# Second stage of a two-layer image kernel: the per-pixel channel contraction is collected densely in one PSUM bank

## The chip, the cores and the metric

One core of a Trainium2 chip runs the whole kernel. The metric is the device time of one execution in microseconds (us); the figure given for the kernel is the median of three runs.

## The reference, cut to what matters

The input `x` has 16 images of 64 channels, 256 x 256 pixels each, in float32 (16 MB an image). Two layers each add a convolution-like term of the normalised image to it:

```python
x = x + L0(_gn(x))     # FFT, mix 16 channels in each of 4 heads on 32 x 17 modes, inverse FFT, + bias
x = x + L1(_gn(x))     # at each pixel, over the 64 channels:
#   alpha = xf[:, 0] * mu[0] - xf[:, 1:] @ mu[1:]     (mu: one vector for the whole batch)
#   alpha = max(alpha, 1 + EPS);  d = arccosh(alpha);  var = mean(d * d)
#   coef = d / sqrt(alpha * alpha - 1);  v = coef * (x - alpha * mu);  ... scaled by 1 / sqrt(var)
```

`_gn` normalises over pairs of channels. The part that this change touches is `alpha`: one weighted sum over 64 channels for each of the 65,536 pixels of an image. The normalised input of layer 1 is x plus a low-frequency field, so the sum splits in two: a weighted sum of the raw x (from DRAM), and the same sum taken on the 32 x 17 modes and brought back to pixels by a small inverse transform.

## The kernel before, in words

The kernel has three stages with a barrier between them. Stage A computes transforms and statistics, stage B (`stage_b`) computes for each pixel the maps derived from `alpha`, and stage C reads x once more and writes the output. Only stage B is changed.

Stage B reads every image once more. An image is cut into T = 8 tiles of 2 MB, `xt`, in NX = 4 buffers: partition p = 2c + s holds half s of channel c, 4096 pixels to a tile. SP issues the loads (`load(b, t)`, L632), and each waits until the tile that had its buffer has been contracted (`al_mm`).

- **PE.** `contract(b, t)` (L650) makes 8 matmuls of 128x512 float32 with a 32-column stationary operand `awc` (weights in columns 0 and 1, one for each half s, zeros in the rest), four into each of two PSUM banks `p_al[k]`, at partitions 0, 32, 64 and 96. Only 2 of the 32 result rows of each carry data. `layer(b)` stands between tiles 6 and 7: the inverse transform along h into `p_z` (L659), a copy by ACT (`zs`), then along w into `p_y[0]` (the alpha part) and `p_y[1]` (channel 0's field), L666.
- **ACT.** `copy_alpha` (L692) copies each bank to `al_r`, twice for a tile; `store_alpha` (L697) writes the rows with data to DRAM (`alx`) after tiles 3 and 7. Between tiles 3 and 4 of image b it runs `distances(b - 1)` (L707 to L715): two square roots, a logarithm and a squared sum, each waiting for DVE.
- **DVE.** For image b: `combine(b)` (L804 to L810) multiplies and sums the modes `spt` (loaded from `spec`) for the layer, then `dense(b - 1)` (L824 to L850) computes the maps of the image before on 128x512 tiles, from `ald` (alpha read back from `alx`) and `x0d` (channel 0). Channel 0 and the maps are laid out with image rows on partitions.
- **POOL.** It issues the small DMAs, in this order for image b: `weights(b)` (L741, waits until image b - 1 is contracted), `load_modes(b)` (L747, two DMAs into the only `spt`), `load_dense(b - 1)` (`x0d`, then `ald` once `alx` is written), `store_dense(b - 1)` (L760 to L762: `maps`, `bmap`, `x10`).

```python
            with dve.Fori(1, B) as b:
                ch.loop(b, 1, PER_B)
                combine(b)
                dense(b - 1)
                ch.end(B - 1)
```

Before the loop DVE runs `combine(0)` and then a long setup of the weights of stage C (L856 to L911). What POOL, SP and PE of one image wait for is counted by semaphores; the order on each engine is the order of the code.

Of the kernel before, what the change touches and what calls it, by code (L numbers as in the profile page):

```python
# [36 lines left out]
def constants():  # L37
# [28 lines left out]
    c["idft_h"] = ih  # L66
    w = 2 * np.pi * ky[:, None] * np.arange(W) / W
# [481 lines left out]
def stage_b(nc, ctx, io, B, keep):  # L549
# [3 lines left out]
    SL = T * TB // (4 * 512)  # L553
    x_v = x.rearrange("b c h w -> b (c h w)").rearrange("b (p t n) -> b t p n", p=128, t=T)
    x0_v = x.rearrange("b c (s h) w -> b c h s w", s=2)
    al_v = io["alx"].rearrange("b s (h w) -> b h s w", w=W)
    al_rows = io["alx"].rearrange("b s (k j n) -> b s j k n", j=4, n=512)
# [3 lines left out]
    al_mm, al_sb = sem("al_mm"), sem("al_sb")  # L561
    al_out = [sem(f"al_out{k}") for k in range(2)]
    al_in, x0_in, sp_in, sp_used = sem("al_in"), sem("x0_in"), sem("sp_in"), sem("sp_used")
# [7 lines left out]
    with ExitStack() as mem:  # L571
# [3 lines left out]
        al_r = sb("al_r", [128, SL, 512])  # L575
# [11 lines left out]
        aw, awc = sb("aw", [128, B, 32]), sb("awc", [128, 32])  # L587
# [10 lines left out]
        ald, x0d, x10, al, t1, t2, w1, w2, dist, coef, beta = (dn[:, k] for k in range(11))  # L598
# [11 lines left out]
        def _(sp):  # L610
# [14 lines left out]
            sp.dma_start(idft_h[:], cst["idft_h"]).then_inc(c_in, 16)  # L625
# [15 lines left out]
        def _(pe):  # L641
            def contract(b, t):

                pe.wait_ge(x_in[t % NX], b * (16 * T // NX) + (t // NX) * 16 + 16)
                for k in range(2):
                    if not (is_at(b, 0) and t == 0):
                        pe.wait_ge(al_sb, b * 2 * T + 2 * t + k - 1)
                    for j in range(4):
                        at = 2048 * k + 512 * j
                        last = nc.tensor.matmul(p_al[k][32 * j:32 * j + 32, :], awc[:], xt[t % NX][:, at:at + 512], start=True, stop=True)  # L650
                    last.then_inc(al_mm, 1)

            def layer(b):
# [8 lines left out]
                if not is_at(b, 0):  # L662
                    pe.wait_ge(alpha, b * 2)
# [20 lines left out]
        def _(act):  # L684
            S = nc.scalar

            def copy_alpha(b, t):
                for k in range(2):
                    act.wait_ge(al_mm, b * 2 * T + 2 * t + k + 1)
                    if t % (T // 2) == 0 and k == 0 and not is_at(b, 0):  # L690
                        act.wait_ge(al_out[2 * t // T], b * 32)
                    S.activation(al_r[:, 2 * t + k], p_al[k][:], ACT.Copy).then_inc(al_sb, 1)  # L692

            def store_alpha(b, half):
                act.wait_ge(al_sb, b * 2 * T + (half + 1) * T)
                for s in range(2):
                    act.dma_start(al_rows[b, s][:, half * T:half * T + T], al_r[s::32, half * T:half * T + T]).then_inc(al_out[half], 16)  # L697

# [688 lines left out]
```

## Time and profile before

| | |
|---|---|
| median of 3 runs | 4943.81 us (4943.03 to 4945.26) |
| profiled execution, its span | 4939.4 us |
| stage A | 0 to 1351.4 us of the span |
| stage B | 1351.4 to 2266 us |
| stage C | 2266 to 4939.4 us |
| PE / DVE / ACT / POOL busy over the span | 77% / 69% / 45% / 30% |
| DMA over the span | 242 GB/s on average |

The profile is of one execution. Its span runs from the first to the last instruction and is 4.4 us under the median of the runs. "Idle before, releaser" tells how long an engine had nothing to do before a group and what ended that. A matmul of float32 shows as more than one record. [...]

### The profile page before, as it was taken

The numbers are of one execution on the slowest core, as the hardware profiler recorded it, in microseconds if no ns is written. First come the engines' busy times: TensorE is split into PE (matmuls) and PEld (weight loads), VectorE is DVE, ScalarE is ACT, GpSimd is POOL, SyncE is SP. The second block draws the span as 40 slices with busy tenths as digits, with TensorE's granted clock in tenths as the row PEclk, the third lists the DMA queues.
The fourth block names the chain that finished last, engine by engine and source line by source line (L and its number), as shares of the span: only waits on it lengthen the run. The fifth ranks groups of instructions, "written<-read, shape, count | busy, mean of one in ns | idle before, by whom it ended". The sixth has DMA issues, their size and how long they took to land.

```text
span 4939.4 us, 72319 instructions
## 1 busy us (share of the span) xinstructions
PE 3805.1 (77%) x23619; PEld 2097.6 (42%) x23874; DVE 3399.5 (69%) x3499; ACT 2240.3 (45%) x3020; POOL 1460.1 (30%) x737
## 2 busy tenths in 40 slices
PE   7777777777144344433999999999999999999998
PEld 3444444444111011002555555555555555555554
DVE  2989889898863433343776677667767776676677
ACT  5555555455022233232554455445554554454544
POOL 0010110101100010001454444444444444444444
PEclk9988888898566677766999999999999999999999
DMA  9565756655099989982777777777777777777776
GB/s 367 192 251 188 258 198 229 228 193 213 14 381 357 364 342 363 351 345 81 224 235 219 227 239 221 224 223 241 224 222 224 237 227 224 227 234 224 223 244 217
DMA packets 288845, 1197.47 MB, mean 242 GB/s; under 512 B 30174, under 2 KB 46846, under 8 KB 205828
## 3 DMA queue, kind: packets, MB, share of 16 engines
q1 hardware_dynamic: 274740, 1151.85, 68.7%
q0 software_dynamic: 11600, 38.32, 2.1%
q10 hardware_dynamic: 2304, 4.20, 0.2%
q8 instruction: 178, 2.92, 0.2%
q14 instruction: 23, 0.19, 0.0%
HBM read 883.32 MB, written 310.94 MB: 242 GB/s over the span
## 4 chain that ended last, share of the span: by engine, by line
PE 50%; issue 3%; DMA 1%; DVE 0%; SPq 0%; POOL 0%; ACT 0%; POOLq 0%; ACTq 0%
PE c_p_u L1129 20%; PE c_p_z L1099 11%; PE c_p_t L1112 10%; PE c_p_p L1153 5%; PE c_p_g L1135 4%; DMA c_mv<-bmap 0%; POOL c_ot L1306 0%; ACT c_zc L1189 0%; DVE c_zc L1280 0%; DMA c_ys<-spec 0%; SPq L1070 0%; DMA c_x<-x 0%; DVE c_rt L1288 0%; SPq L1069 0%; PE c_p_z L1174 0%
## 5 line engine op out<-in xcount | busy, mean ns | idle before, releaser
L1306 POOL TENSOR_TENSOR c_ot<-c_s,c_u 128x1024 f32<-128x1024 f32 x512 | 1211.3, 2366 | 1411.6 <-DVE c_s L1259 1411.6
L1189 ACT ACTIVATE c_zc<-c_p_z 34x512 f32<-34x512 f32 x512 | 546.4, 1067 | 1316.0 <-PE c_p_z L1099 1261.5
L1250 DVE TENSOR_TENSOR c_u<-c_xt,c_p_u 128x1024 f32<-128x1024 f32 x512 | 625.3, 1221 | 745.0 <-PE c_p_u L1129 722.5
L1129 PE MATMUL c_p_u<-c_mv,c_zc 128*128 128x256 f32 x4096 | 1043.7, 399 | 76.5 <-issue 75.5
L1129 PEld LDWEIGHTS c_p_u<-c_mv,c_zc 128*128 128x128 f32 x4096 | 750.7, 193 | 590.1 <-issue 465.7
L650 PE MATMUL b_p_al<-b_xt,b_awc 128*32 128x512 f32 x2048 | 333.9, 791 | 502.6 <-ACT b_al_r L692 314.9
L1259 DVE SCALAR_TENSOR_TENSOR c_s<-c_u,keep_k,c_p_g 128x1024 f32<-128x1024 f32 x512 | 655.8, 1281 | 18.0
L1269 DVE TENSOR_TENSOR c_ot<-c_ot,c_p_p 128x1024 f32<-128x1024 f32 x512 | 621.4, 1214 | 1.8 <-POOL c_ot L1306 1.3
L1218 ACT ACTIVATE c_sq<-c_s,c_btcol 128x1024 f32<-128x1024 f32 x512 | 589.2, 1151 | 52.8 <-DVE c_s L1259 22.3
L1099 PEld LDWEIGHTS c_p_z<-c_idft_h,c_ys 128*34 128x34 f32 x8176 | 477.6, 113 | 224.7 <-issue 215.2
L1099 PE MATMUL c_p_z<-c_idft_h,c_ys 128*34 128x64 f32 x8176 | 559.6, 222 | 7.8 <-ACT c_zc L1189 7.8
L329 ACT ACTIVATE a_junk<-a_xt 128x1024 bf16<-128x1024 f32 x512 | 534.4, 1049 | 31.1 <-DMA a_xt<-in_x 23.7
L1112 PE MATMUL c_p_t<-c_sq,c_halves 128*32 128x512 f32 x2048 | 538.7, 605 | 0.0
L248 PE MATMUL a_p_rows<-a_xt,a_dft_h 128*64 128x512 f32 x2048 | 504.5, 638 | 34.2 <-DMA a_bias_t<-in_bias 19.6
L391 DVE TENSOR_REDUCE a_y<-a_prod 128x34 f32<-128x1088 f32 x256 | 502.7, 2005 | 5.7
L336 ACT ACTIVATE a_rows<-a_p_rows 128x512 f32<-128x512 f32 x256 | 151.4, 591 | 532.9 <-PE a_p_rows L248 532.9
L650 PEld LDWEIGHTS b_p_al<-b_xt,b_awc 128*32 128x32 f32 x2048 | 65.0, 130 | 760.7 <-ACT b_al_r L692 426.9
L804 DVE TENSOR_TENSOR b_prod<-b_spt,b_arow 64x2176 f32<-64x2176 f32 x16 | 38.7, 2418 | 474.6 <-DMA b_spt<-spec 474.2
L515 POOL TENSOR_TENSOR a_sm<-a_sm 128x8 f32<-128x8 f32 x16 | 26.8, 1675 | 1138.1 <-DVE a_sm L452 1138.1
L692 ACT ACTIVATE b_al_r<-b_p_al 128x512 f32<-128x512 f32 x256 | 149.3, 595 | 404.6 <-PE b_p_al L650 404.5
L386 DVE TENSOR_TENSOR a_prod<-a_wm,a_xh 128x1088 f32<-128x1088 f32 x256 | 317.9, 1283 | 0.3
L261 PE MATMUL a_p_tr<-a_ident,a_rows 128*128 128x128 f32 x1024 | 163.5, 297 | 189.1 <-DVE a_cols L374 177.1
(177 smaller groups left out, 3090.8 us busy)
## 6 DMA issues: line engine op xcount, KB each, us to landing
a_xt<-in_x SPq DMA_DIRECT2D x256, 1024.0 KB, 9.7
b_xt<-in_x SPq DMA_DIRECT2D x128, 2048.0 KB, 18.9
c_xt<-in_x SPq DMA_DIRECT2D x256, 1024.0 KB, 6.4
out<-c_ot SPq DMA_DIRECT2D x256, 1024.0 KB, 8.5
maps<-b_maps POOLq DMA_DIRECT2D x16, 768.0 KB, 14.9
c_rt<-maps SPq DMA_DIRECT2D x256, 48.0 KB
a_wm<-in_wmix SPq DMA_DIRECT2D x1, 8704.0 KB, 34.9
b_spt<-spec POOLq DMA_DIRECT2D x32, 272.0 KB, 23.4
```

Of the source, the lines that this page charges most:

```text
L248: last = nc.tensor.matmul(p_rows[i][64 * t:64 * t + 64, :], dft_h[:, j], xt[q % NX][:, t::2, i, j * W:(j + 1) * W], start=(j == 0), stop=( ...
L329: nc.scalar.activation(junk[h % 2][:].rearrange("p (i w) -> p i w", i=2), xt[q % NX][:, h], ACT.Square, accum_out=sq[:, q, h:h + 1]).then_ ...
L391: ch.inc(V.tensor_reduce(y[:, o].rearrange("p (a k) -> p a k", a=2), prod[o % 2][:].rearrange("p a (n k) -> p a k n", k=KY), AX_X, ALU.add))
L1099: last = nc.tensor.matmul(p_z[0:M2, 64 * c:64 * c + 64], ys[:, 8 * part + c], idft_h[:].rearrange("p (s h) -> p s h", s=2)[:, :, 32 * chun ...
L1112: last = nc.tensor.matmul(p_t[at:at + 32, :], halves[:], sq[n][:, 512 * j:512 * j + 512], start=True, stop=True)
L1129: ins = nc.tensor.matmul(p_u[:, W * r:W * r + W], zc[ck % 2][:, (t % TCH) * ROWS + row], mv[t % 2][:, W * row:W * row + W], start=True, st ...
L1189: S.activation(zc[chunk_buffer][0:M2, :, 16 * part:16 * part + 16].rearrange("m h c -> m c h"), p_z[0:M2, :].rearrange("m (c h) -> m c h", ...
L1218: S.activation(sq[n][:], s0[n][:], ACT.Square, bias=btcol[:]).then_inc(sq_done, 1)
L1250: V.tensor_tensor(u[n][:], xt[t % 4][:, 1024 * n:1024 * n + 1024], p_u[:], ALU.add).then_inc(u_done, 1)
L1259: V.scalar_tensor_tensor(out=s0[n][:], in0=u[n][:], scalar=keep["k"][:], in1=p_g[:], op0=ALU.mult, op1=ALU.mult).then_inc(s_done, 1)
L1269: V.tensor_tensor(o, o, p_p[:], ALU.add).then_inc(o_done, 1)
L1306: P.tensor_tensor(ot[t % 4][:, 1024 * n:1024 * n + 1024], s0[n][:], u[n][:], ALU.add).then_inc(v_done, 1)
```

## The change

- `contract` writes all matmuls of an image into one bank `p_al`, four column groups as before. The stationary operand is a window of 32 columns of a 47-column `awc` that has weights in columns 15 and 31: for pixel block k the window starts at 15 - k, so the two data rows land on rows k and 16 + k of each group, and the other rows get zeros added. After 16 blocks the bank holds the alpha of all pixels of the image, dense. The first block starts the accumulation, the rest add to it.
- The layer's alpha part is accumulated into the same bank; channel 0's field goes to one bank `p_y`. A reordered constant, `idft_d`, gives both in the new order of pixels.
- `copy_alpha`, `store_alpha`, the `alx` tensor, `ald` and the waits on them are gone. DVE reads `p_al` itself and counts `al_read`; PE waits for it before tile 0 of the next image. There is one `p_al` where there were two banks used in turn.
- `dense` starts with the operation on `p_al` (one operation fewer); ACT's work for an image is `copy_z(b)`, then `distances(b)`.
- Channel 0, `maps`, `bmap` and `x10` are moved in four DMAs of 32 partitions instead of one of 128; runs in DRAM are twice as long. `load_dense(b)` is now issued in image b's own turn, after `load_modes(b)`.

```diff
             def load(b, t):
                 if not (is_at(b, 0) and t < NX):
-                    sp.wait_ge(al_mm, b * 2 * T + 2 * (t - NX) + 2)
+                    sp.wait_ge(al_mm, b * T + t - NX + 1)
                 sp.dma_start(xt[t % NX][:], x_v[b, t]).then_inc(x_in[t % NX], 16)
...
                 pe.wait_ge(x_in[t % NX], b * (16 * T // NX) + (t // NX) * 16 + 16)
-                for k in range(2):
-                    if not (is_at(b, 0) and t == 0):
-                        pe.wait_ge(al_sb, b * 2 * T + 2 * t + k - 1)
-                    for j in range(4):
-                        at = 2048 * k + 512 * j
-                        last = nc.tensor.matmul(p_al[k][32 * j:32 * j + 32, :], awc[:], xt[t % NX][:, at:at + 512], start=True, stop=True)
-                    last.then_inc(al_mm, 1)
+                if t == 0 and not is_at(b, 0):
+                    pe.wait_ge(al_read, b)
+                for e in range(8):
+                    k, j = 2 * t + e // 4, e % 4
+                    last = nc.tensor.matmul(p_al[32 * j:32 * j + 32, :], awc[:, 15 - k:47 - k], xt[t % NX][:, 512 * e:512 * e + 512],
+                                            start=(k == 0), stop=False, skip_group_check=True)
+                last.then_inc(al_mm, 1)
...
-                for q in range(2):
-                    for s in range(2):
-                        last = nc.tensor.matmul(p_y[q][:, 256 * s:256 * s + 256], zs[:, q, 128 * s:128 * s + 128], idft_w[0:M2], start=True, stop=True)
+                for r in range(2):
+                    nc.tensor.matmul(p_y[:, 256 * r:256 * r + 256], zs[:, 1, HD * r:HD * r + HD], idft_w[0:M2], start=True, stop=True)
+                for r in range(2):
+                    last = nc.tensor.matmul(p_al[:, 256 * r:256 * r + 256], zs[:, 0, HD * r:HD * r + HD], idft_w[0:M2],
+                                            start=False, stop=False, skip_group_check=True)
...
             def entry(b):
-                for t in range(T):
-                    copy_alpha(b, t)
-                    if t == T // 2 - 1:
-                        store_alpha(b, 0)
-                        if not is_at(b, 0):
-                            distances(b - 1)
-                    if t == T - 2:
-                        copy_z(b)
-                store_alpha(b, 1)
+                copy_z(b)
+                distances(b)
...
             def load_dense(b):
                 if not is_at(b, 0):
-                    pool.wait_ge(alpha, b * 2)
-                pool.dma_start(x0d[:].rearrange("p (s w) -> p s w", s=2), x0_v[b, 0]).then_inc(x0_in, 16)
-                for half in range(2):
-                    pool.wait_ge(al_out[half], b * 32 + 32)
-                pool.dma_start(ald[:].rearrange("p (s w) -> p s w", s=2), al_v[b]).then_inc(al_in, 16)
+                    pool.wait_ge(alpha, b)
+                for j in range(4):
+                    pool.dma_start(x0d[32 * j:32 * j + 32], x0_v[b, 0, j]).then_inc(x0_in, 16)
...
             def store_dense(b):
                 pool.wait_ge(maps_ready, b + 1)
-                pool.dma_start(io["maps"][b].rearrange("m s (h w) -> h (m s) w", w=W), maps[:].rearrange("p m (s w) -> p (m s) w", s=2)).then_inc(maps_out, 16)
-                pool.dma_start(io["bmap"][b].rearrange("s (h w) -> h s w", w=W), beta[:].rearrange("p (s w) -> p s w", s=2)).then_inc(beta_out, 16)
-                pool.dma_start(io["x10"][b].rearrange("s (h w) -> h s w", w=W), x10[:].rearrange("p (s w) -> p s w", s=2)).then_inc(x10_out, 16)
+                for j in range(4):
+                    at = slice(32 * j, 32 * j + 32)
+                    pool.dma_start(maps_v[b, j], maps[at]).then_inc(maps_out, 16)
+                    pool.dma_start(dense_v(io["bmap"])[b, j], beta[at]).then_inc(beta_out, 16)
+                    pool.dma_start(dense_v(io["x10"])[b, j], x10[at]).then_inc(x10_out, 16)
...
             def entry(b):
                 weights(b)
                 load_modes(b)
-                load_dense(b - 1)
+                load_dense(b)
                 store_dense(b - 1)
...
-                V.scalar_tensor_tensor(out=x10[:], in0=x0d[:], scalar=brow[:, 0:1], in1=p_y[1][:], op0=ALU.add, op1=ALU.add).then_inc(alpha, 1)
-                V.tensor_tensor(t1[:], ald[:], p_y[0][:], ALU.add).then_inc(alpha, 1)
-                dve.wait_ge(alpha, b * 2 + 2)
-                ch.step(V.tensor_scalar(al[:], t1[:], col(ac, b), 1.0 + EPS, ALU.add, ALU.max))
+                V.tensor_scalar(al[:], p_al[:], col(ac, b), 1.0 + EPS, ALU.add, ALU.max).then_inc(al_read, 1)
+                V.scalar_tensor_tensor(out=x10[:], in0=x0d[:], scalar=brow[:, 0:1], in1=p_y[:], op0=ALU.add, op1=ALU.add).then_inc(alpha, 1)
+                dve.wait_ge(al_read, b + 1)
```

## Rows read from the trace of the kernel before

**Rows 1.** Stage B: busy of PE, PEld, DVE, ACT, POOL; clock, DMA share, GB/s.

```profile
1351.40:2269.00 917.60, 381.80 (x2242) 94.20 (x2242) 386.21 (x431) 260.93 (x399) 90.20 (x136) 0.70 0.88 341
```

**Rows 2.** Waits, stage B: engine, line, releaser: total us, times, longest.

```profile
DVE b_prod L804 <- DMA b_spt<-spec: 474.2, 15, 34.2
...
PE b_p_al L650 <- ACT b_al_r L692: 314.9, 46, 20.3
```

**Rows 3.** Combine's first multiply, by source line: duration, first and last start.

```profile
L804 DVE TENSOR_TENSOR b_prod<-b_spt,b_arow x16: 2417/2418/2419, 1383.2 to 2207.7; 64x2176 f32<-64x2176 f32 x16
```

**Rows 4.** Timeline, steady period: start, us, engine, line, operation, [idle before <- releaser].

```profile
1515.78 24.97 SPq L632 DMA_DIRECT2D b_xt<-in_x  x7
...
1523.21 0.21 POOL L741 COPY b_awc<-b_aw 128x32 f32 x1 [1.93 <-PE b_p_al L650]
...
1523.94 1.22 POOL L747 DMA_DIRECT2D b_spt<-spec  x2 [0.53 <-issue]
...
1536.76 3.39 PE L650 MATMUL b_p_al<-b_xt,b_awc 128*32 128x512 f32 x16 [4.70 <-DMA b_xt<-in_x]
...
1551.20 2.42 DVE L804 TENSOR_TENSOR b_prod<-b_spt,b_arow 64x2176 f32<-64x2176 f32 x1 [33.11 <-DMA b_spt<-spec]
...
1558.77 0.75 DVE L824 SCALAR_TENSOR_TENSOR b_dn<-b_dn,b_brow,b_p_y 128x512 f32<-128x512 f32 x1 [0.70 <-DMA b_dn<-alx]
...
1566.53 5.58 PE L650 MATMUL b_p_al<-b_xt,b_awc 128*32 128x512 f32 x32 [18.16 <-ACT b_al_r L692]
...
1572.04 1.05 PE L659 MATMUL b_p_z<-b_idft_h,b_vm 128*34 128x256 f32 x4
...
1577.83 0.20 POOL L741 COPY b_awc<-b_aw 128x32 f32 x1 [1.92 <-PE b_p_al L650]
```

**Rows 5.** Two windows of that period; columns as in rows 1.

```profile
1508.00:1512.00 4.00, 0.12 (x4) 0.12 (x8) 3.93 (x4) 3.83 (x7) 0.00 (x0) 0.50 0.86 365
1512.00:1516.00 4.00, 4.00 (x20) 0.82 (x24) 3.86 (x7) 1.32 (x3) 0.00 (x0) 0.52 0.12 49
```

**Rows 6.** DMA issues, stage B: count, KB, median us to landing.

```profile
b_spt<-spec POOLq DMA_DIRECT2D x32, 272.0 KB, 23.4
...
x<-b_dn POOLq DMA_DIRECT2D x16, 256.0 KB, 21.2
```

**Rows 7.** Tile view of xt: its matmuls (ns; first, last start), landing times.

```profile
L650 PE MATMUL b_p_al<-b_xt,b_awc x2048: 592/617/1063, 1370.9 to 2232.9; 128*32 128x512 f32 x187
...
DMA to landing us min/median/max: 7.2/18.9/29.4
```

**Rows 8.** Timeline of the start of stage B, image 0.

```profile
1368.85 1.18 POOL L747 DMA_DIRECT2D b_spt<-spec  x2
...
1383.17 2.42 DVE L804 TENSOR_TENSOR b_prod<-b_spt,b_arow 64x2176 f32<-64x2176 f32 x1 [8.99 <-DMA b_spt<-spec]
...
1384.91 3.64 PE L650 MATMUL b_p_al<-b_xt,b_awc 128*32 128x512 f32 x16 [3.08 <-DMA b_xt<-in_x]
...
1399.60 3.48 PE L650 MATMUL b_p_al<-b_xt,b_awc 128*32 128x512 f32 x16 [2.97 <-DMA b_xt<-in_x]
```

**Rows 9.** Timeline of image 1's combine and image 0's dense.

```profile
1442.69 2.42 DVE L804 TENSOR_TENSOR b_prod<-b_spt,b_arow 64x2176 f32<-64x2176 f32 x1 [0.33 <-DVE keep_lw L869]
...
1449.97 0.75 DVE L824 SCALAR_TENSOR_TENSOR b_dn<-b_dn,b_brow,b_p_y 128x512 f32<-128x512 f32 x1 [0.41 <-DVE b_sc L810]
```

**Rows 10.** Timeline: end of stage B, first operation of stage C.

```profile
2231.54 1.92 PE L650 MATMUL b_p_al<-b_xt,b_awc 128*32 128x512 f32 x16
...
2243.03 0.75 DVE L824 SCALAR_TENSOR_TENSOR b_dn<-b_dn,b_brow,b_p_y 128x512 f32<-128x512 f32 x1 [14.12 <-DMA b_dn<-alx]
...
2258.05 1.04 POOL L760 DMA_DIRECT2D maps<-b_maps  x1 [17.54 <-issue]
...
2259.79 0.73 POOL L762 DMA_DIRECT2D x<-b_dn  x1
...
2266.11 3.55 POOL L1323 MEMSET c_mv<- 128x2048 f32 x2 [4.98 <-POOLq L571]
```

More of the change, by code:

```diff
@@ L552, in stage_b @@
     NX, T = 4, HALF // TB
-    SL = T * TB // (4 * 512)
+    HD = 128
     x_v = x.rearrange("b c h w -> b (c h w)").rearrange("b (p t n) -> b t p n", p=128, t=T)
-    x0_v = x.rearrange("b c (s h) w -> b c h s w", s=2)
-    al_v = io["alx"].rearrange("b s (h w) -> b h s w", w=W)
-    al_rows = io["alx"].rearrange("b s (k j n) -> b s j k n", j=4, n=512)
+    x0_v = x.rearrange("b c (q j r) w -> b c j q (r w)", j=4, r=2)
+    dense_v = lambda a: a.rearrange("b s (k j n) -> b j (s k) n", j=4, n=512)
+    maps_v = io["maps"].rearrange("b m s (k j n) -> b j (s k) m n", j=4, n=512)
     x_in = [sem(f"x_in{k}") for k in range(NX)]
@@ L560, in stage_b @@
     mm_done, pow_done, mean_ready = sem("mm_done"), sem("pow_done"), sem("mean_ready")
-    al_mm, al_sb = sem("al_mm"), sem("al_sb")
-    al_out = [sem(f"al_out{k}") for k in range(2)]
-    al_in, x0_in, sp_in, sp_used = sem("al_in"), sem("x0_in"), sem("sp_in"), sem("sp_used")
+    al_mm, al_read = sem("al_mm"), sem("al_read")
+    x0_in, sp_in, sp_used = sem("x0_in"), sem("sp_in"), sem("sp_used")
     v_ready, z_mm, z_sb, y_mm = sem("v_ready"), sem("z_mm"), sem("z_sb"), sem("y_mm")
@@ L586, in stage_b @@
         arow = sb("arow", [128, B, C])
-        aw, awc = sb("aw", [128, B, 32]), sb("awc", [128, 32])
+        aw, awc = sb("aw", [128, B, 2]), sb("awc", [128, 47])
         ac, q2, q3, dsum = sb("ac", [128, B]), sb("q2", [128, B]), sb("q3", [128, B]), sb("dsum", [128, B])
@@ L597, in stage_b @@
         dn = sb("dn", [128, 11, 512])
-        ald, x0d, x10, al, t1, t2, w1, w2, dist, coef, beta = (dn[:, k] for k in range(11))
+        _, x0d, x10, al, t1, t2, w1, w2, dist, coef, beta = (dn[:, k] for k in range(11))
         wide = dn[:, 4:8].rearrange("p k n -> p (k n)")[:, 0:2 * B * C].rearrange("p (b c s) -> p b c s", b=B, s=2)
@@ L602, in stage_b @@
         maps = sb("maps", [128, 6, 512], BF16)
-        p_al = [ps(f"p_al{k}", [128, 512]) for k in range(2)]
+        p_al = ps("p_al", [128, 512])
         p_z = ps("p_z", [128, 512])
-        p_y = [ps(f"p_y{k}", [128, 512]) for k in range(2)]
+        p_y = ps("p_y", [128, 512])
         p_v = ps("p_v", [128, 512])
@@ L685, in _ @@
             S = nc.scalar
[L687 to L697, printed above, removed]
             def copy_z(b):
@@ L731, in _ @@
                 entry(b)
-            distances(B - 1)
         @block.gpsimd
@@ L739, in weights @@
                 if not is_at(b, 0):
-                    pool.wait_ge(al_mm, b * 2 * T)
-                P.tensor_copy(awc[:], aw[:, b]).then_inc(w_ready, 1)
+                    pool.wait_ge(al_mm, b * T)
+                P.tensor_copy(awc[:, 15:47:16], aw[:, b]).then_inc(w_ready, 1)
             def load_modes(b):
@@ L778, in _ @@
             load_modes(0)
+            load_dense(0)
             pool.wait_ge(uw_ready, 1)
@@ L872, in _ @@
             ch.inc(V.memset(btrow[:, 0:1], 0.0))
-            ch.inc(V.memset(aw[:], 0.0))
+            ch.inc(V.memset(awc[:], 0.0))
             ch.inc(V.memset(vm[:], 0.0))
@@ L1340, in program @@
         io["macc"] = dram("macc", (HEADS, CI))
-        io["alx"] = dram("alx", (B, 2, HALF))
         io["x10"] = dram("x10", (B, 2, HALF))
```

26 lines of the change are left out of this document (13 added, 13 removed).

## Prediction, written before the changed kernel ran

> **What bounds the kernel now.** I read the windows by stage first. Stage B, the only one that the change touches, is a third of the work in length but has DMA busy for 0.88 of its time at 341 GB/s, while PE is busy for 382 of 918 us and DVE for 386 [rows 1]. That looks like a stage bound by its loads. Two further views say that this is not the whole answer. In the waits, DVE stands for 474 us before combine because the modes `spt` have not landed, up to 34 us at a time, and PE stands for 315 us behind ACT's copies [rows 2]. And in each period there is a hole: of two windows of 4 us one has DMA at 0.86, the next at 0.12 [rows 5], which makes 4.1 us without loads.
>
> The period is 54.6 us: combine of image 1 starts at 1442.7 [rows 9], that of image 15 at 2207.7 [rows 3], 14 periods in 765 us. The timeline of one period shows what closes it [rows 4]. I call t0 the end of an image's last contraction, just before `weights` at 1523.2.
> - t0 to the start of combine, 28.1 us: POOL waits for t0 before `load_modes`; its two DMAs are issued by 1525.2 and have landed at 1551.2.
> - combine to PE's restart, 15.3 us: combine, `dense` of the image before, and ACT's `distances` inside its row of copies (1551.2 to 1566.5).
> - restart to the next t0, 11.2 us: two tiles in 5.6 us, then layer and one tile in another 5.6.
>
> The sum is 54.6. So the period is a ring of latencies, PE to POOL to DMA to DVE to ACT to PE, that happens to stand close to what the loads need. After the restart only tiles 5 to 7 are left to contract, and all of them are in their buffers.
>
> **The change, part by part.**
>
> *ACT's copies, `alx`, `ald` go.* 256 copies, 64 stores and 16 loads. The 15.3 us section loses what stood behind ACT: it now ends with the first operation of `dense`. What DVE does in combine stays. The `alx` traffic (0.26 MB written and read for each image, beside some 19 MB) is worth 1 or 2 us of DMA time in a period; as the new ring is not filled by DMA, I count it as nothing, and it would count if DMA closed the ring.
>
> *The new wait.* PE may not start tile 0 of image b before DVE has read `p_al` of b - 1. DVE's order is combine(b), dense(b - 1). combine(b) needs `spt` of b, whose load POOL issues only after t0 of b - 1. So the whole of an image's contraction now lies behind the landing of its modes; before, tiles 0 to 4 of it ran in that time. Behind the waiting PE stand SP's loads, since a buffer comes free only by a contraction: four tiles are loaded ahead, and then the load queue dries out. The new ring has four terms. S is the moment when PE starts an image.
>
> 1. S to t0, all eight tiles. Tiles 0 to 3 are there. The first takes 3.6 us at the lower clock, 0.50 after the wait [rows 5, 8]; then tile 4 is issued, at S + 3.9. A load into an idle queue takes 7.2 us at least [rows 7], so it lands at S + 11.1. Undisturbed, tiles follow 4.9 us apart (three from 1384.9 to 1399.6) [rows 8]. Beside POOL's stores they take 6.9: three tiles from the issue at 1515.8 to 1536.8 are 21.0, less 7.2, over two [rows 4]. The stores start some 13 us after S (`dense` takes 15.0 us to its first store [rows 10], less what went before S). I take 4.9 for tile 5, 6.9 for 6 and 7: tile 6 lands at S + 22.9. Its contraction takes 3.6 us; layer and tile 7 take 5.6 at the full clock [rows 4], and I take 8.1 at the lower one, as 3.64 against 1.92 us for the tile alone says [rows 8, 10]. That makes 34.6 us. Ends: 28.4 with 4.9 throughout and a full clock, 36.6 with 6.9 throughout.
> 2. t0 to the issue of the second `spt` DMA: 2.1 us, as now [rows 4].
> 3. Its landing. With an empty POOL queue but x loads beside it: 13.1 us (1370.0 to 1383.2) [rows 8]. Behind the three stores: 26.0 us [rows 4]. In the new order the stores are issued from S + 13 and t0 comes at S + 35, so they have 22 us; now the last of them lands 21.2 us after its issue [rows 6]. They are just about through. I take 15, near the lower end, with 13.1 and 26.0 as ends.
> 4. combine, 7.6 us (1551.2 to 1558.8) [rows 4], then the read of `p_al`, one operation not above 0.75 [rows 4], and its signal: 8.4 us. No end is far from it.
>
> The period is 34.6 + 2.1 + 15 + 8.4 = 60.1 us, 5.5 more than now. All low ends together give 52.0, all high ends 73.1.
>
> *The stores in four parts.* Twelve DMAs in place of three, and four for channel 0. An issue of this size costs POOL 0.6 us (1.22 for two) [rows 4], so about 7 us in place of 2.5. In the ring this lies between S + 13 and S + 22, before t0, and costs nothing; if t0 came before S + 22, `weights` and `spt` would be late by it. At the end of the stage nothing covers it.
>
> [...] The parts are 64 KB, those of `maps` 192 KB. The rows have nothing smaller than the 64 KB of `alx`, and no effect of its size can be read from the rows above. [...]
>
> *Matmuls.* As many as before, same shape, same four column groups; only where they write and that they add. I cost this at nothing; the bound above is that adding to one bank keeps the groups from overlapping, a rival below. The window of `awc` and the layer's new order change no size.
>
> *First and last image.* `combine(1)` still starts at 1442.7, since the setup of stage C's weights sets it [rows 9]; `dense(0)` starts at 1450.0, so S of image 1 is 1450.8. At the end, the trip over `alx` goes: now t0 at 2233.5 is followed by `dense` at 2243.0, its first store at 2258.05, the last at 2259.8, and stage C at 2266.1 [rows 10]. Then: t0 + 0.3, `dense` to the stores 14.3 (15.0 less the dropped 0.7), 7 us of issues, and 5.6 from there to stage C: 27.2 us in place of 32.6.
>
> **The sum.** S of image 15 is 1450.8 + 14 x 60.1 = 2292.2; t0 is 2326.8; stage C starts at 2354.0 instead of 2266.1, 87.9 us later. Stages A and C are the same work. The profiled execution's own time, 4939.4, becomes 5027.3. The median of the runs stands 4.4 us above that span: 5031.7. A microsecond of period is 14 us of time, and the change breaks even at a period of 53.8 us.
>
> **The rivals.**
> - *The buffers hide the wait (faster).* If four loaded tiles carry DMA over PE's wait, DMA closes the ring: 54.6 less the hole of 4.1 is 50.5 us, stage C starts at 2219.6, and the time is 4897. It needs PE back within about 18 us of t0, while tiles 1 to 3 of the next image still land (three at 6 us). For it speaks the high DMA share; against it that term 3 and 4 alone make 23.4, and with both at their low ends still 21.5. It decides at a period under 53.8, so nearly all low ends must come together. 8 in 100.
> - *A milder ring.* Loads less disturbed, `spt` at 13: period 55.5, time 4967. 9 in 100.
> - *POOL's queue is slower in parts.* If the stores in parts are not through when `spt` is issued, `spt` lands in 20 us instead of 15, halfway to the present 26: period 65.1, stage C at 2424, time 5102. For it: POOL's DMAs do wait for each other and for x loads, 13.1 against 26.0. [...] Against it: the stores have 22 us. 17 in 100.
> - *Column groups no longer overlap.* 16 records of 0.617 us for a tile [rows 7] one after another are 9.9 us, eight tiles and the layer some 85 us, period 110, time about 5790. Nothing in the rows speaks for it. 2 in 100.
> - *The likeliest*, period 57 to 63: 4988 to 5074. 60 in 100. The rest, 4 in 100, is what I have not thought of.
>
> **How the numbers follow.** The time is 5032. For 8 in 10 I go from a period of 56.1 to the queue rival: 4975 to 5105. Differences under 0.2%, 10 us, can't be told from none here; a period of 53.1 to 54.5 would give that. Faster by more: 0.09. Within: 0.03. Slower by more: 0.88.
>
> **What would show it.** In the profile after: PE's longest waits ended by DVE's first operation of `dense`, 15 times and some 25 us each with the rest of idle time on DMA; DMA at nothing for about 10 us of each period, share in stage B near 0.8; combine 60 us apart; `spt` landing about 15 us after its issue; layer at tile 6 not waiting. DVE's wait for `spt` stays the largest. The prediction is wrong if the x queue never dries, if t0 comes later than S + 37 (tiles slower than 6.9), or if `spt` lands as late as now.

## The result and the profile after

| | median | runs | against the kernel before |
|---|---|---|---|
| kernel before | 4943.42 us | 4935.26 to 4945.26, 4 runs | |
| changed kernel | 4976.59 us | 4969.14 to 4979.09, 4 runs | 1.0068, 95% interval 1.0053 to 1.0082 |

The change makes the kernel 33 us slower. The forecast was slower by 88 us: the direction is right, the size is 2.7 times too large. The median lies 1.6 us inside the low end of the forecast range (4975 to 5105). The profiled execution took 4969.1 us with a span of 4967.6, the shortest of its four runs, so its span shows 28 us where the medians show 33.

The windows by stage of the changed kernel (columns as in [rows 1]):

```profile
1351.40:2295.00 943.60, 382.50 (x2242) 103.24 (x2242) 375.42 (x410) 93.81 (x128) 157.96 (x307) 0.67 0.83 323
```

Stage B is 26 us longer in these bounds (stage C starts 30.9 us later, see below), with DMA at 0.83 and 323 GB/s where [rows 1] have 0.88 and 341. ACT's work fell from 261 to 94 us and the bytes fell too, and the stage is longer all the same. Two waits of stage B, from the view of waits (columns as in [rows 2]):

```profile
DVE b_prod L785 <- DMA b_spt<-spec: 505.7, 15, 36.8
...
PE b_p_al L648 <- DVE b_dn L805: 372.3, 15, 34.8
```

PE's wait for ACT's copies [rows 2] has gone. In its place stands a wait for DVE's first operation of `dense` (L805), once for each of images 1 to 15, 25 us on average. DVE's own wait for the modes is longer than before, 506 us against 474. One whole period in the timeline of the changed kernel:

```profile
1563.93 9.45 PE L648 MATMUL b_p_al<-b_xt,b_awc 128*32 128x512 f32 x64 [23.69 <-DVE b_dn L805]
...
1575.12 1.92 PE L648 MATMUL b_p_al<-b_xt,b_awc 128*32 128x512 f32 x16 [1.74 <-DMA b_xt<-in_x]
...
1580.02 1.93 PE L648 MATMUL b_p_al<-b_xt,b_awc 128*32 128x512 f32 x16 [2.97 <-DMA b_xt<-in_x]
...
1585.72 3.60 PE L648 MATMUL b_p_al<-b_xt,b_awc 128*32 128x512 f32 x16 [3.78 <-DMA b_xt<-in_x]
...
1589.25 1.05 PE L658 MATMUL b_p_z<-b_idft_h,b_vm 128*34 128x256 f32 x4
...
1593.09 3.37 PE L648 MATMUL b_p_al<-b_xt,b_awc 128*32 128x512 f32 x16
...
1596.69 0.19 POOL L722 COPY b_awc<-b_aw 128x2 f32 x1 [12.64 <-PE b_p_al L648]
1597.40 1.21 POOL L728 DMA_DIRECT2D b_spt<-spec  x2 [0.53 <-issue]
1611.66 2.42 DVE L785 TENSOR_TENSOR b_prod<-b_spt,b_arow 64x2176 f32<-64x2176 f32 x1 [35.25 <-DMA b_spt<-spec]
...
1619.11 0.75 DVE L805 TENSOR_SCALAR b_dn<-b_p_al,b_ac 128x512 f32<-128x512 f32 x1 [0.58 <-DVE b_sc L791]
...
1620.01 8.72 PE L648 MATMUL b_p_al<-b_xt,b_awc 128*32 128x512 f32 x64 [23.54 <-DVE b_dn L805]
```

It is to be read as the ring of the forecast. PE starts at 1563.9 right behind the read of `p_al`, contracts four tiles that were there, then takes tiles 4 to 6 as they land (1575.1, 1580.0, 1585.7), the layer, and tile 7. t0 is at 1596.5; `weights`, then the two DMAs of the modes; they have landed 13.1 us after the last issue; combine; the read; PE starts at 1620.0. The terms are 32.6 + 2.1 + 13.1 + 8.3 = 56.1 us, where the ring before took 54.6 [rows 3, 4, 9]. Two sections got shorter: t0 to combine 15.2 us instead of 28.1, combine to PE's restart 8.3 instead of 15.3, where PE had stood behind ACT. The third, restart to t0, grew from 11.2 to 32.6, since all eight tiles lie in it now, and that is more than the two saved. Combine's first multiply gives the mean: image 1's starts at 1441.6, image 15's at 2229.4, so 56.3 us for each of 14 periods. From the view by source line:

```profile
L785 DVE TENSOR_TENSOR b_prod<-b_spt,b_arow x16: 2416/2416/2418, 1382.1 to 2229.4; 64x2176 f32<-64x2176 f32 x16
```

and from the timeline, image 1:

```profile
1441.64 2.42 DVE L785 TENSOR_TENSOR b_prod<-b_spt,b_arow 64x2176 f32<-64x2176 f32 x1 [0.33 <-DVE keep_lw L850]
```

How long the DMAs of the modes take to land, over all images, from the tile view of `spt`:

```profile
DMA to landing us min/median/max: 9.3/12.5/15.8
```

Windows of 4 us of that period (columns as in [rows 5]): the first two hold the layer and tile 7, the last three, at the end of the period, show the dry load queue:

```profile
1588.00:1592.00 4.00, 3.32 (x17) 1.27 (x10) 0.00 (x0) 1.64 (x2) 0.00 (x0) 0.84 0.96 402
1592.00:1596.00 4.00, 4.00 (x21) 1.11 (x19) 0.00 (x0) 0.23 (x1) 0.00 (x0) 0.58 1.05 446
...
1612.00:1616.00 4.00, 0.00 (x0) 0.00 (x0) 3.97 (x2) 0.00 (x0) 0.00 (x0) 0.50 0.78 332
1616.00:1620.00 4.00, 0.00 (x0) 0.02 (x1) 3.35 (x5) 0.00 (x0) 0.00 (x0) 0.50 0.00 0
1620.00:1624.00 4.00, 3.99 (x24) 1.18 (x28) 3.80 (x7) 2.48 (x3) 2.02 (x4) 0.58 0.15 47
```

In the last 12 us DMA stands for 8.3 by its shares (0.22, 1.00 and 0.85 of 4 us), against 4.1 before [rows 5]. The end of the stage in the timeline of the changed kernel:

```profile
2237.75 8.75 PE L648 MATMUL b_p_al<-b_xt,b_awc 128*32 128x512 f32 x64 [24.67 <-DVE b_dn L805]
...
2270.71 0.75 DVE L805 TENSOR_SCALAR b_dn<-b_p_al,b_ac 128x512 f32<-128x512 f32 x1 [20.47 <-PE b_p_al L648]
...
2284.28 0.59 POOL L741 DMA_DIRECT2D maps<-b_maps  x1 [26.42 <-DVE b_maps L831]
...
2290.05 0.50 POOL L743 DMA_DIRECT2D x<-b_dn  x1
...
2297.01 3.55 POOL L1304 MEMSET c_mv<- 128x2048 f32 x2 [5.86 <-POOLq L571]
```

`dense` of the last image now follows its contraction at once (before: 9.5 us later, over `alx` [rows 10]). Twelve stores take POOL 6.3 us. Stage C starts at 2297.0 instead of 2266.1, 30.9 us later; stage C itself is 2.7 us shorter in this execution.

### The profile page after: what moved, and what is told of

It is laid out like the page before. It is cut to its first block, busy times and chain, and to the rows that moved or that the text cites. A ratio compares the mean times of both kernels' runs of the same rounds, so it can differ in the third digit from the quotient of the medians.

```text
span 4967.6 us, 72010 instructions
## 1 busy us (share of the span) xinstructions
PE 3854.0 (78%) x23874; PEld 2112.6 (43%) x23874; DVE 3391.0 (68%) x3483; ACT 2070.9 (42%) x2749; POOL 1529.9 (31%) x913
## 4 chain that ended last, share of the span: by engine, by line
PE 51%; issue 1%; DMA 0%; DVE 0%; SPq 0%; ACT 0%; POOLq 0%; DVEq 0%; ACTq 0%
PE c_p_u L1110 20%; PE c_p_z L1080 11%; PE c_p_t L1093 10%; PE c_p_p L1134 6%; PE c_p_g L1116 5%; DMA c_mv<-bmap 0%; DMA c_ys<-spec 0%; ACT c_zc L1170 0%; DVE c_zc L1261 0%; SPq L1051 0%; DMA c_x<-x 0%; DVE c_rt L1269 0%; SPq L1050 0%; PE c_p_z L1155 0%; DVE c_ys L1262 0%
## 5 line engine op out<-in xcount | busy, mean ns | idle before, releaser
L1134 PE MATMUL c_p_p<-c_rt,keep_lw 128*128 128x512 bf16 x1024 | 310.2, 385 | 1.9 <-DVE c_ot L1250 1.9
L1116 PE MATMUL c_p_g<-c_rt,keep_lw 128*128 128x512 bf16 x1024 | 310.3, 385 | 0.0
```

Source lines behind the costliest of these rows:

```text
L1116: ins = nc.tensor.matmul(p_g[:, 512 * k:512 * k + 512], lw(0, b), rt[t % 2][:, at:at + 512], start=True, stop=True)
L1134: ins = nc.tensor.matmul(p_p[:, 512 * k:512 * k + 512], lw(1, b), rt[t % 2][:, at:at + 512], start=True, stop=True)
```

## Experiments

Two theories stood against each other. *The wait*: the loss is PE's wait for the read of `p_al`, which stands on DVE behind a combine whose modes are loaded only after the contraction, and so the load queue runs dry. *The parts*: the loss is in the small DMAs. A third, slower matmuls into one bank, was tested along. Differences are between the medians, each to runs of the kernel before taken with it (medians 4938.3 to 4941.5 us); the changed kernel is at +33.

| run | median | difference | ratio, 95% interval |
|---|---|---|---|
| modes_early | 4859.56 us | -79 | 0.9841 (0.9825 to 0.9858) |
| dense_first | 4852.81 us | -85 | 0.9829 (0.9813 to 0.9845) |
| two_banks | 4863.83 us | -78 | 0.9843 (0.9826 to 0.9859) |
| unrolled | 4977.44 us | +36 | 1.0069 (1.0054 to 1.0084) |
| modes_twice | 5102.21 us | +161 | 1.0325 (1.0308 to 1.0342) |
| before_parts | 5010.23 us | +72 | 1.0145 (1.0128 to 1.0162) |
| before_no_alx | 4913.89 us | -24 | 0.9949 (0.9933 to 0.9966) |
| first_modes_twice | 4919.67 us | -22 | 0.9952 (0.9935 to 0.9968) |
| first_extra_plain | 4924.71 us | -17 | 0.9961 (0.9946 to 0.9977) |
| first_extra_wide | 4881.62 us | -60 | 0.9875 (0.9860 to 0.9890) |
| first_stores_twice | 4944.96 us | +3 | 1.0011 (1.0001 to 1.0020) |
| best | 4837.58 us | -104 | 0.9795 (0.9781 to 0.9808) |

### modes_early: the modes are loaded before they are waited for

In POOL's `entry(b)`; the modes of image 1 are loaded after `load_dense(0)`:

```diff
                 weights(b)
-                load_modes(b)
                 load_dense(b)
+                if not last:
+                    load_modes(b + 1)
                 store_dense(b - 1)
```

> Changed kernel, with one reordering on POOL: the modes of the next image are loaded right after channel 0's, before the stores, and no longer after the end of the image's contraction. If the lost time is PE's wait for the read of p_al behind combine and the modes' landing (about 15.5 us from the last contraction to combine), combine is done before the contraction ends, PE restarts about 1 us after it, the load queue never runs dry, and the period falls from 56.3 us to what DMA needs, 48 to 51 us: about 80 to 110 us less than the changed kernel, near 4880, and faster than the kernel before. If the loss is the bytes or the number of the small DMAs, they are the same here: period 55 to 57, time within 15 us of the changed kernel. If it is slower matmuls into one bank, the same.

Measured: 79 us under the kernel before, 112 under the changed one. A window inside stage B (columns as in [rows 1]) has DMA at full share:

```profile
1480.00:2060.00 580.00, 335.83 (x1688) 76.20 (x1690) 238.49 (x265) 70.35 (x97) 116.21 (x228) 0.70 1.01 395
```

The small DMAs, the bytes and the matmuls are those of the changed kernel. The wait carries the loss. The time is some 20 us under what was expected: DMA closes the period at 47.2 us, not at 48 to 51.

### dense_first: the order on DVE

```diff
-                combine(b)
                 dense(b - 1)
+                combine(b)
```

> Changed kernel, with one reordering on DVE: in the loop dense(b - 1) comes before combine(b); the modes are still loaded after the contraction's end. If PE's wait is one of order (the read of p_al stands behind combine), PE restarts 1 us after the last contraction and the period falls to 48 to 51 us, time near 4880, although the modes land as late as before. If the landing of the modes by itself closes the ring (through the layer at tile 6), the period stays above 54 and the time above 4940.

Measured: 85 us under the kernel before, with the modes loaded as late as in the changed kernel. In its timeline PE's tile 0 follows the last contraction with the read between them, 1.1 us of idle time:

```profile
1569.52 1.92 PE L648 MATMUL b_p_al<-b_xt,b_awc 128*32 128x512 f32 x16
...
1571.61 0.75 DVE L805 TENSOR_SCALAR b_dn<-b_p_al,b_ac 128x512 f32<-128x512 f32 x1 [24.78 <-PE b_p_al L648]
...
1572.37 1.21 POOL L728 DMA_DIRECT2D b_spt<-spec  x2 [0.53 <-issue]
...
1572.51 1.92 PE L648 MATMUL b_p_al<-b_xt,b_awc 128*32 128x512 f32 x16 [1.07 <-DVE b_dn L805]
```

So it is not the landing by itself, nor the one bank by itself, but the order: the read of `p_al` had no need of combine(b) and stood behind it. From here on this kernel serves as a base in which DMA is what closes the period: from 1480 to 2060 its share is 1.01 at 394 GB/s, and image 1 to image 14 take 660.9 us, 47.2 each.

### two_banks and unrolled

```diff
-        p_al = ps("p_al", [128, 512])
+        p_als = [ps(f"p_al{k}", [128, 512]) for k in range(2)]
...
-                if t == 0 and not is_at(b, 0):
-                    pe.wait_ge(al_read, b)
+                p_al = p_als[b % 2]
+                if t == 0 and b > 1:
+                    pe.wait_ge(al_read, b - 1)
```

> Changed kernel with two banks for alpha used in turn by odd and even images, so that tile 0 waits for the read of the image before the last (the loops over images of PE and DVE are written out for it). If the one bank together with the order on DVE makes the wait, PE goes on without it, the load queue does not dry out and the period is 48 to 51 us, time 4850 to 4890. If the late modes stop PE at the layer all the same, the period stays above 54.

`unrolled` has only the loops over images of PE and DVE written out, as two_banks needs them.

> Changed kernel with the loops over images of PE and DVE written out, nothing else: the control for two_banks. Same order, same waits: period 56 to 57 us, time within 15 us of the changed kernel's 4977. If writing them out was what sped two_banks up, it is near 4864.

Measured: two_banks -78 us, unrolled +36, within 3 us of the changed kernel (+33). A second bank takes the wait away as well, and writing the loops out does nothing. `unrolled` also repeats the changed kernel's result.

### modes_twice: a dose of the suspected term

```diff
+                for k in range(2):
+                    pool.dma_start(extra[KX * k:KX * k + KX].rearrange("k (h i) m -> k h (i m)", h=HEADS),
+                                   spec[b, k].rearrange("(h k) n -> k h n", h=HEADS)).then_inc(sp_in, 16)
                 for k in range(2):
                     pool.dma_start(spt[KX * k:KX * k + KX].rearrange("k (h i) m -> k h (i m)", h=HEADS),
```

> Changed kernel, with the modes loaded twice (two more DMAs of the same bytes into a tile of their own, ahead of the real ones). If their landing after the contraction's end is a term of the ring, the period grows by the added landing, from 56.3 to 62 to 67 us, and the time by 80 to 150 us over the changed kernel. If DMA volume closes the ring, the 0.56 MB cost 1.3 us at 430 GB/s: period 57.6, time 20 us over. If neither: no change.

Measured: 128 us over the changed kernel. From its timeline, the issues after t0:

```profile
1621.88 0.19 POOL L723 COPY b_awc<-b_aw 128x2 f32 x1 [12.95 <-PE b_p_al L649]
1622.59 1.21 POOL L729 DMA_DIRECT2D b_extra<-spec  x2 [0.53 <-issue]
1623.79 1.09 POOL L732 DMA_DIRECT2D b_spt<-spec  x2
```

and the landing and PE's restart:

```profile
1645.28 2.42 DVE L789 TENSOR_TENSOR b_prod<-b_spt,b_arow 64x2176 f32<-64x2176 f32 x1 [43.98 <-DMA b_spt<-spec]
...
1653.63 9.75 PE L649 MATMUL b_p_al<-b_xt,b_awc 128*32 128x512 f32 x64 [31.96 <-DVE b_dn L809]
```

The modes land 20.4 us after the last issue instead of 13.1, and 1.1 us more go into issues: 8.4 us a period by these lines. By combine's starts the period is 64.9 us instead of 56.3, 8.6 more, and image 1's combine starts 8.6 us later as well (1450.3), since the setup on DVE stands behind combine(0): 15 times 8.6 are 129. The ring is as drawn.

### before_parts: the stores in parts, alone

`bmap` and `x10` are cut in the same way.

```diff
-                pool.dma_start(io["maps"][b].rearrange("m s (h w) -> h (m s) w", w=W), maps[:].rearrange("p m (s w) -> p (m s) w", s=2)).then_inc(maps_out, 16)
+                for j in range(4):
+                    at = slice(32 * j, 32 * j + 32)
+                    pool.dma_start(io["maps"][b].rearrange("m s (h w) -> h (m s) w", w=W)[at], maps[at].rearrange("p m (s w) -> p (m s) w", s=2)).then_inc(maps_out, 16)
...
```

> Kernel before, with its three stores of 128 partitions cut into twelve of 32, nothing else. POOL's issues take 7 us in place of 2.5, and here they stand right before the contraction's end, so the modes are issued some 2.5 us later: period 57, time about 35 us over the kernel before, if the parts cost nothing in the DMA queue. If the parts hold the queue longer, the modes land more than 26 us after their issue (28 to 31) and the period is 59 to 62, time 60 to 100 us over. If POOL's issues are hidden: no change.

Measured: +72 us, in the second range. Combine's first multiply, by source line:

```profile
L806 DVE TENSOR_TENSOR b_prod<-b_spt,b_arow x16: 2417/2418/2420, 1381.4 to 2271.9; 64x2176 f32<-64x2176 f32 x16
```

Image 1's starts at 1440.9, so the period is 59.4 us, 4.7 more than before; 14 of them make 66 us, and 6 more pass between the last combine and stage C, where twelve issues stand. From its timeline, the first store, tile 7, `weights`, the modes and combine:

```profile
1582.84 0.64 POOL L762 DMA_DIRECT2D maps<-b_maps  x1 [35.40 <-DVE b_maps L852]
...
1586.06 1.92 PE L650 MATMUL b_p_al<-b_xt,b_awc 128*32 128x512 f32 x16
...
1589.86 0.21 POOL L741 COPY b_awc<-b_aw 128x32 f32 x1
...
1590.58 1.20 POOL L747 DMA_DIRECT2D b_spt<-spec  x2 [0.51 <-issue]
...
1619.91 2.42 DVE L806 TENSOR_TENSOR b_prod<-b_spt,b_arow 64x2176 f32<-64x2176 f32 x1 [37.81 <-DMA b_spt<-spec]
```

t0 is at 1588.0, but POOL comes to `weights` only at 1589.9, with its issues between: 1.8 us later than before. From the last modes' issue to combine it is 28.1 us instead of 26.0 [rows 4]. The two tiles after the longer wait take 6.6 us instead of 5.6. That is 4.9 in this period. So behind twelve stores the modes land some 2 us later. Two causes can make that, and the run does not separate them: parts hold the queue longer, or the last store merely has less of a lead, since its issue ends 0.8 us before the modes' begins, where these were 2.7 us in the kernel before. Either way it is far from the 5 us that the queue rival put on the changed kernel, where the stores are issued 20 us ahead and are out of the way when the modes come.

### before_no_alx: what the round trip cost

```diff
-                store_alpha(b, 1)
...
-                pool.dma_start(ald[:].rearrange("p (s w) -> p s w", s=2), al_v[b]).then_inc(al_in, 16)
...
+            ch.inc(V.memset(ald[:], 1.0))
```

> Kernel before, without the writes and the read of alx (alpha is taken as a constant 1 in the maps; copies by ACT stay). It tells what slowed the x tiles to 6.9 us behind PE's restart: if the stores of POOL did it, the third tile still comes 21 us after the first load's issue; if the alx writes did it, 17 to 19 us. The period itself should stay at 53.5 to 54.6 us, since the ring of waits does not pass alx: time within 15 us of the kernel before. If alx traffic was what bound the stage, the period falls by 3 us or more and the time by 45.

Measured: -24 us, outside the 15 that were given for it. From its timeline, the first load after PE's restart, the modes' issue, the third tile and combine:

```profile
1565.70 63.20 SPq L632 DMA_DIRECT2D b_xt<-in_x  x12
...
1574.41 1.21 POOL L743 DMA_DIRECT2D b_spt<-spec  x2 [0.50 <-issue]
...
1585.52 3.64 PE L650 MATMUL b_p_al<-b_xt,b_awc 128*32 128x512 f32 x16 [4.25 <-DMA b_xt<-in_x]
...
1599.80 2.42 DVE L797 TENSOR_TENSOR b_prod<-b_spt,b_arow 64x2176 f32<-64x2176 f32 x1 [31.79 <-DMA b_spt<-spec]
```

The third tile comes 19.8 us after the first issue instead of 21.0, between what the two cases gave, so `alx` accounts for a part of the 6.9 us pace only. The modes land 24.2 us after their last issue instead of 26.0: the round trip did touch the ring, through the modes' landing, by 1.8 us a period (52.8 instead of 54.6 by combine's starts). The forecast had counted this traffic as nothing, on the ground that DMA does not fill the ring; it costs all the same where it delays a landing that is in the ring.

### first_modes_twice, first_extra_plain, first_extra_wide: what slows the tiles

All three on the kernel with dense first, where added DMA time shows in full. The second load of modes is as above; the other two load as many bytes from x, after the modes, first_extra_plain (first lines) into 64 partitions in rows of 8704 B, first_extra_wide (last lines) into 128 in pieces of 2176 B:

```diff
+                for k in range(2):
+                    pool.dma_start(extra[KX * k:KX * k + KX], x_v[0, 0][KX * k:KX * k + KX, 0:C * M2]).then_inc(sp_in, 16)
...
+                for k in range(2):
+                    pool.dma_start(extra[:, 544 * k:544 * k + 544], x_v[0, 0][:, 544 * k:544 * k + 544]).then_inc(sp_in, 16)
```

> The kernel with dense first (period 48.5 us, DMA at full share all through), modes loaded twice: what the modes' load costs the DMA engines. In its windows the rate falls from 430 to 320 GB/s for some 16 us while they are in flight, which makes 4 us lost and 1.3 us for their own bytes: period up by 5.4, time by 80 us. If they cost their bytes alone: 1.3 us, 20 us.

> The kernel with dense first, with an extra load of as many bytes as the modes into the same 64 partitions, in whole rows of 8704 B (from x) instead of pieces of 2176 B. Doubling the modes cost 67 us. If the pieces' size and place in DRAM make them dear, this costs little over its bytes: 20 to 35 us. If it is that 64 partitions are written, that is, half of the memory's width, it costs 55 to 75 us.

> As first_extra_plain, but pieces of 2176 B over all 128 partitions. If the number of partitions makes the modes dear: 20 to 35 us. If the short pieces do: 55 to 75 us.

Measured against dense_first, each by its difference to the kernel before: +64, +69 and +26 us. The first is under the 80 that were expected, the other two fall where "64 partitions" had put them. Not all of this is DMA time in the period. combine(0) waits for the added load too, and the setup on DVE stands behind it, so PE starts image 1 later; the end is longer as well. What images 1 to 14 take, from PE's first matmul of image 1 (timeline) to the last `weights` (tile view of `awc`), in the profiled execution of each:

| run | image 1 starts | last `weights` | 14 images | more, for one image |
|---|---|---|---|---|
| dense_first | 1442.4 | 2103.3 | 660.9 us | |
| first_modes_twice | 1452.0 | 2169.8 | 717.8 us | 4.1 us |
| first_extra_plain | 1451.4 | 2167.4 | 716.0 us | 3.9 us |
| first_extra_wide | 1449.9 | 2128.6 | 678.7 us | 1.3 us |

The runs of one kernel differ by up to 16 us, about 1 us for an image, so 4.1 and 3.9 are the same. 0.56 MB at the 430 GB/s that dense_first moves beside stores (426 to 434 in its windows from 1592 to 1608) are 1.3 us: the wide load costs its bytes, the narrow ones three times as much. With DMA at full share in all of them, the rates say it again, first_extra_plain and then first_extra_wide:

```profile
1480.00:2060.00 580.00, 307.70 (x1544) 69.17 (x1545) 217.61 (x242) 65.18 (x89) 119.45 (x231) 0.69 1.01 372
...
1480.00:2060.00 580.00, 326.90 (x1634) 72.77 (x1636) 237.31 (x264) 68.49 (x94) 130.28 (x252) 0.69 1.01 391
```

So neither the short pieces nor their place in `spec` make the modes dear, but how many partitions the load writes. Two things changed together there and were not separated: the two DMAs of the modes write 64 partitions in all and 32 each, those of the wide load 128 each. The windows of 4 us of dense_first (columns as in [rows 5]) show it from the other side, one with only stores beside the x tiles, then four behind the modes' issue (1573.6), all with DMA near full share:

```profile
1548.00:1552.00 4.00, 2.05 (x12) 0.59 (x16) 0.00 (x0) 0.00 (x0) 0.00 (x0) 0.50 1.05 445
...
1576.00:1580.00 4.00, 2.86 (x16) 0.58 (x16) 3.94 (x2) 2.00 (x4) 0.00 (x0) 0.67 1.05 319
1580.00:1584.00 4.00, 0.64 (x4) 0.00 (x0) 3.83 (x9) 0.00 (x0) 0.00 (x0) 0.91 1.02 299
1584.00:1588.00 4.00, 2.30 (x12) 0.60 (x16) 2.00 (x3) 0.00 (x0) 2.10 (x4) 0.52 1.00 334
1588.00:1592.00 4.00, 1.34 (x8) 0.00 (x0) 3.97 (x2) 0.00 (x0) 3.71 (x8) 0.50 0.99 323
```

The modes have landed at 1587.0. In the last window it is channel 0's four loads of 32 partitions each that can still be in flight: they were issued by 1575.9 and land 15.6 us after their issue in the median. Beside the stores, which read 32 partitions each, the rate holds (426 to 434 GB/s from 1592 to 1608), so they cost about their bytes: tiles 3 to 6 of that image are contracted 5.8 us apart (1592.7 to 1610.1), and these 17.4 us at 430 GB/s are 7.5 MB, three tiles of 2.1 MB and 1.2 of the stores' 1.31 MB.

### first_stores_twice: not conclusive for the stores' price

`bmap` and `x10` are doubled in the same way, to DRAM tensors of their own.

```diff
                     pool.dma_start(maps_v[b, j], maps[at]).then_inc(maps_out, 16)
+                    pool.dma_start(maps2_v[b, j], maps[at]).then_inc(maps_out, 16)
...
```

> The kernel with dense first, maps, bmap and x10 stored twice (24 stores in 32-partition parts): what the stores cost the DMA engines. With only stores beside them the windows show 410 to 455 GB/s and x tiles 5.8 us apart instead of 4.9. If they cost their bytes, 1.31 MB at 430 GB/s: 3 us a period, time up by 45 us. If they had slowed the tiles to 6.9 us, as the forecast's first term has it: 8 to 10 us a period, 120 to 150 us.

Measured: 89 us over dense_first, between the two expectations, and by another cause than either. From its timeline, tiles 5 and 6, `weights`, and the next read of `p_al`:

```profile
1565.44 1.92 PE L649 MATMUL b_p_al<-b_xt,b_awc 128*32 128x512 f32 x16 [2.96 <-DMA b_xt<-in_x]
...
1571.22 3.56 PE L649 MATMUL b_p_al<-b_xt,b_awc 128*32 128x512 f32 x16 [3.85 <-DMA b_xt<-in_x]
...
1580.49 0.19 POOL L723 COPY b_awc<-b_aw 128x2 f32 x1 [4.48 <-PE b_p_al L649]
...
1601.94 0.75 DVE L809 TENSOR_SCALAR b_dn<-b_p_al,b_ac 128x512 f32<-128x512 f32 x1 [32.78 <-DMA x<-b_dn]
```

`dense` waits until the stores of the image before have landed, and with 24 of them that is 21.6 us after t0: a new ring, so the price of the stores can't be taken from the total. What can be read is the pace: tile 6 is contracted 5.8 us after tile 5 with stores in flight, as in the changed kernel (5.7).

### best

`dense(0)` moves between the parts of DVE's setup; SP issues the last image's stores of `bmap` and `x10` after its last load, and POOL keeps those of `maps`.

```diff
+            dense(0)
             ch.step(V.tensor_tensor(v2[:], srow[:, :, 1], over_b(btrow[:]), ALU.add))
...
+            combine(1)
-            with dve.Fori(1, B) as b:
-                ch.loop(b, 1, PER_B)
+            with dve.Fori(2, B) as b:
+                ch.loop(b, 2, PER_B)
                 dense(b - 1)
                 combine(b)
...
+            sp.wait_ge(maps_ready, B)
```

> The kernel with dense first, and two more steps: dense(0) moved into the setup of stage C's weights, so that PE can start image 1 some 25 us earlier (now it waits until about 1443 us, and the load queue runs dry from 1424 on), and the last image's stores of bmap and x10 issued by SP beside POOL's. Period as before, 48 us; the start gains 15 to 22 us, the end 2 to 4: time 4828 to 4836. If the start was hidden (DMA makes up for it later), it stays at 4850.

Measured: 104 us under the kernel before (0.9795), 18 under dense_first, and 2 us over the range that was given; stage C starts at 2158.0 instead of 2176.4. Image 1 starts at 1414.1 instead of 1442.4, but its layer then waits 8.7 us for combine(1), since the setup lies between. From its timeline, image 1's first tile and its layer:

```profile
1414.07 1.92 PE L654 MATMUL b_p_al<-b_xt,b_awc 128*32 128x512 f32 x16 [1.07 <-DVE b_dn L814]
...
1464.08 1.92 PE L664 MATMUL b_p_z<-b_idft_h,b_vm 128*34 128x256 f32 x4 [8.70 <-DVE b_vm L798]
```

## Why the forecast was right in kind and wrong in size

- **The ring.** Right: the four terms are in the trace, and the links that close it were taken out or stretched one by one: the order (dense_first), the landing (modes_early, modes_twice), the bank (two_banks). PE's wait, 15 times and 25 us each, and the dry queue (8.3 us of a period, where 10 were given) are in the profile.
- **The step that failed: the sum of the period, "34.6 + 2.1 + 15 + 8.4 = 60.1".** It measured 56.3. Two of its terms were too large, term 1 by 2.0 us and term 3 by 1.9; terms 2 and 4 came out within 0.1 us.
- **Term 1, 34.6, measured 32.6.** Tiles 4 and 5 came as given, at S + 11.2 and S + 16.1. Tile 6 came at S + 21.8, not 22.9: "Beside POOL's stores they take 6.9" was a wrong reading of [rows 4]. Stores, modes, channel 0's load and `alx` were all in flight in that stretch. Stores alone lift the pace from 4.9 to 5.7 or 5.8 us. `alx` was worth 1.2 us over three tiles (before_no_alx). The modes, dear by the few partitions that they write (3.9 us against 1.3 for as many bytes, first_extra_plain against first_extra_wide), fit the rest; in the kernel before itself they were not taken out. In the changed kernel neither modes nor `alx` are in flight between S and t0. The rest of the term, 0.9 us, is the layer and tile 7: 7.2 us, where 8.1 were taken. The rows named for it, 3.64 against 1.92 us, add 1.7 to the 5.6 and give 7.3; the other 0.8 had no row. The granted clock, a share of the full one, stood at 0.84 and then at 0.58 there, not throughout at 0.50, the lower clock of the forecast (windows above).
- **Term 3, 15, measured 13.1** in the period shown, the lower end: the stores were through. Over all images no DMA of the modes took more than 15.8 us to land. What the queue rival feared of the parts is at most some 2 us right behind twelve stores (28.1 for 26.0 us, before_parts), where its cause was not separated, and here nothing; no run shows that DMA takes longer over a store for its being cut into parts of 64 or 192 KB.
- **How it adds up.** The 14 periods took 787.8 us where 14 x 60.1 = 841.4 were given, 53.6 less. Image 1 started 0.8 us earlier than given, the last image's term 1 was 1.9 shorter (2237.8 to 2270.5), the end 0.7 shorter (26.5 for 27.2). Sum 57.0, which is 87.9 less 30.9. Stage C was 2.7 us shorter, which makes 59.7 between the spans, 5027.3 and 4967.6. Between the medians it is 55, since the median stands 9.0 us above the profiled span and not 4.4: that step of the forecast was wrong too, and happened to hide 5 us.
- **Why a small error made a large one.** The forecast change is, for the most part, 14 times a difference of two numbers near 55. An error of 7% of the period is six tenths of the forecast change. The forecast gave this itself (a microsecond of period is 14 us of time), yet its likeliest case began at 57. For the landing it added 1.9 us for safety to the row that was nearest in kind, the one without stores ahead; for the tiles it took a stretch with other traffic in it for one with stores alone.
- **The rivals.** "The buffers hide the wait" is refuted: the wait is not hidden, and taking it away gives 111 to 119 us. What it gave as its time, 4897, is 37 to 44 us more than what modes_early and dense_first reach, since it took the DMA-bound period as 50.5 and it is 47.2. The queue in parts and groups without overlap are refuted for this kernel (landing 15.8 us at most where the rival had 20; four tiles in 9.5 us where it had 9.9 for one). The result fell between the milder ring (55.5, time 4967) and the low end of the likeliest case (57, time 4988). The milder ring's period does not follow from its own terms: 4.9 throughout, the lower clock and 13 for the landing sum to 56.1. That this is what the period shown took is partly luck, since tile 6 was 0.9 us later than that pace gives and the layer with tile 7 0.9 us shorter. The upper end of the likeliest case is 5072 by the forecast's sum, not 5074.
- **The tail and ACT.** 6.1 us were saved at the end, where 5.4 were given. Of ACT's 167 us of saved work only what had stood in the ring counted, the 7.0 us between combine and PE's restart, as given. The `alx` traffic was counted as nothing; in the kernel before it was worth 1.8 us a period, and in the forecast it sat unseen in the pace of 6.9.

## What to carry to other kernels

When two buffers become one, the reader of that buffer becomes a gate for its writer, and everything that stands before the reader in its engine's order is then in the path: look there first, and put the read ahead of work that it does not need (here one swapped pair of lines is worth 119 us). Where a stage is a ring of latencies, write its terms down with a row each and take for each the row that is nearest in kind, not a middle value for safety, since the error is multiplied by the number of turns. If engines' busy times fall and the time does not, ask which term of the ring they were in.

## What the runs showed of the hardware

A load of 0.56 MB into 64 partitions, by two DMAs of 32 each, took 3.9 to 4.1 us in a period that DMA closes, in pieces of 2176 B as in rows of 8704 B (first_modes_twice, first_extra_plain); the same bytes in pieces of 2176 B over 128 partitions took 1.3 us (first_extra_wide). In dense_first the 16 engines moved 299 to 334 GB/s in the four windows behind the modes' issue (1576 to 1592, DMA share 0.99 to 1.05), with such loads or channel 0's of 32 partitions in flight, and 406 to 455 beside x tiles and stores alone (1544 to 1576 and 1592 to 1620, share 0.95 to 1.07). In this kernel the busy share of DMA is then no measure of bytes. Whether that comes of writing half of the partitions or of DMAs that write only 32 each was not separated here, and no run shows what in the chip makes it.

Twelve issues of 32 partitions cost POOL 0.50 to 0.59 us each (changed kernel), three of 128 partitions 0.71 to 1.06 us (kernel before).
